# A state-space layer and its experts on one core: readout vector C spread in bfloat16 parts, the sixth state on GpSimd, and a reordered opening

## What is computed

```python
def step(h, inp):                       # per token t
    dA_t, dB_t, x_t, C_t, t = inp
    h = h * dA_t + dB_t * x_t[:, :, None]
    nrm = jnp.sqrt(jnp.sum(h * h, axis=(1, 2), keepdims=True))
    fac = jnp.minimum(20.0 / (nrm + 1e-08), 1.0)
    h = jnp.where(t % 10 == 0, h * fac, h)          # every tenth token the state is rescaled
    y = jnp.einsum('bdn,bn->bd', h, C_t) + D_param * x_t
    return (h, y)
x_out = x_ssm * (gate * jax.nn.sigmoid(gate)) @ W_out.T
# then: softmax router over 16 experts, top 1, capacity 256 tokens each,
# h = relu(tokens @ w1[e]); out = h @ w2[e], weighted by the gate and added to x
```

## Time and profile before

| | before |
|---|---|
| median of 3 runs | 745.5 us (743.75 to 746.16) |
| the profiled execution: device time, and span in the trace | 746.58 us, 744.9 us |
| mean granted clock of TensorE | 0.935 of full |
| busy, share of the span | PE 85%, PEld 63%, DVE 81%, ACT 78%, POOL 81% |
| costliest groups | DVE scans L1360 318.2 us; POOL products L842 299.2 us; ACT tanh L1076 237.5 us; PE state sums L1722 214.5 us; PE spread of C L1712 101.2 us |
| chain that ended last | PE 29%, DVE 20%, POOL 18%, issue 16%, ACT 12%, DMA 3% |
| stages in the trace | first scan at 38.3 us; segments to 618 us; last logits and routing to 653.7 us; experts to 739.3 us |

### The profile page before, as it was taken

The page is one execution under the profiler, slowest core; times in us unless marked ns, Lnnn a source line. Parts: engine busy times, 40 slices in busy tenths (PEclk is TensorE's granted clock), DMA queues, the critical chain, the costliest instruction groups (busy, mean ns, idle before and its releaser), DMA issues.

```text
span 744.9 us, 12724 instructions
## 1 busy us (share of the span) xinstructions
PE 632.3 (85%) x3892; PEld 467.7 (63%) x3892; DVE 601.7 (81%) x972; ACT 582.1 (78%) x1217; POOL 602.4 (81%) x600
## 2 busy tenths in 40 slices
PE   6787899989989998998999899999978885179974
PEld 3335566667667666666667666766767765168864
DVE  5788799999999999999899999999997974742321
ACT  3797989989999999999999998999988642223330
POOL 4288699999999999999899999999897871167775
PEclk9879799999999999999999999999988897579998
DMA  4340333126134322613441352334124302235652
GB/s 119 100 149 2 129 96 112 55 84 192 52 122 141 105 64 79 192 58 109 110 139 45 100 166 86 99 85 148 49 73 135 78 3 65 70 108 181 202 168 66
DMA packets 59168, 77.03 MB, mean 103 GB/s; under 512 B 13514, under 2 KB 46060, under 8 KB 59104
## 3 DMA queue, kind: packets, MB, share of 16 engines
q1 hardware_dynamic: 55328, 69.92, 31.1%
q0 software_dynamic: 2560, 6.08, 2.6%
q10 hardware_dynamic: 1216, 0.27, 0.2%
HBM read 64.70 MB, written 11.77 MB: 103 GB/s over the span
## 4 chain that ended last, share of the span: by engine, by line
PE 29%; DVE 20%; POOL 18%; issue 16%; ACT 12%; DMA 3%; POOLq 0%; SPq 0%; DVEq 0%; ACTq 0%
DVE h L1360 10%; PE ps L1722 9%; POOL h L842 7%; ACT z L1076 6%; PE ps L1615 3%; PE ps L1712 3%; POOL h L856 3%; PE ps L1697 3%; ACT ps L966 2%; POOL nrm L867 2%; PE ps L581 2%; PE ps L594 2%; DVE bst L1244 2%; POOL h L863 1%; DVE h L1334 1%
## 5 line engine op out<-in xcount | busy, mean ns | idle before, releaser
L1360 DVE TENSOR_TENSOR_SCAN h<-ps,h 128x902 f32<-128x902 f32 x204 | 318.2, 1608 | 16.3 <-ACT ps L966 8.4
L842 POOL TENSOR_TENSOR h<-u,scr 128x640 f32<-128x640 f32 x208 | 299.2, 1471 | 1.7
L1076 ACT ACTIVATE z<-dtb,asc 128x240 f32<-128x240 f32 x576 | 237.5, 485 | 1.0 <-DVE dtb L1301 0.7
L1722 PEld LDWEIGHTS ps<-h,ident 128*128 128x128 f32 x1428 | 208.7, 198 | 24.7 <-issue 13.8
L1722 PE MATMUL ps<-h,ident 128*128 128x160 f32 x1428 | 214.5, 310 | 3.6 <-DVE h L1411 3.2
L966 ACT ACTIVATE ps<-z 128x820 f32<-128x820 f32 (+1 forms) x208 | 139.6, 691 | 29.0 <-DVE h L1360 20.4
L1411 DVE TENSOR_TENSOR h<-h,ps 128x800 f32<-128x800 f32 (+4 forms) x161 | 116.5, 725 | 6.7 <-PE ps L1712 5.9
L1712 PE MATMUL ps<-cdg,ones_w 128*128 128x480 f32 x208 | 101.2, 578 | 0.0
L856 POOL TENSOR_TENSOR h<-h,scr 128x800 f32<-128x800 f32 (+1 forms) x52 | 89.7, 1725 | 0.7 <-DVE h L1376 0.7
L1615 PE MATMUL ps<-xnT,wT 128*128 128x488 f32 x144 | 73.7, 624 | 1.1 <-DVE xnT L1472 0.8
L867 POOL TENSOR_TENSOR nrm<-s,half_e 8x1 f32<-8x1 f32 x52 | 33.1, 636 | 46.8 <-DVE s L1323 46.5
(11 more groups left out here) (196 smaller groups left out, 854.1 us busy)
## 6 DMA issues: line engine op xcount, KB each, us to landing
scr<-b_d SPq DMA_DIRECT2D x52, 640.0 KB, 4.4
scr<-c_d SPq DMA_DIRECT2D x52, 200.0 KB, 4.3
z<-in_L_ffn_w_dram SPq DMA_DIRECT2D x32, 256.0 KB, 3.0
xx_d<-xx SPq DMA_DIRECT2D x8, 256.0 KB, 2.0
xxr<-xx_d SPq DMA_DIRECT2D x8, 256.0 KB, 2.6
cdg<-cdg_d SPq DMA_DIRECT2D x52, 37.8 KB
rows_d<-h2b SPq DMA_DIRECT2D x16, 120.0 KB, 2.1
rows_d<-xxr SPq DMA_DIRECT2D x16, 120.0 KB, 2.2
```

Of the source, the lines that this page charges most:

```text
L842: pool.tensor_tensor(o.rearrange("p (n b) t -> p n b t", b=B), us.unsqueeze(1).to_broadcast([P, nn, B, SEG]), bb[:, S % RING, n0 * BS:(n0 ...
L1076: ins = act.activation(zrow[:, k, :, t0:t1], dtb[:, v % 2, hf, :].rearrange("p (b c) -> p b c", b=B)[:, :, 1 + t0:1 + t1], ACT.Tanh, scale ...
L1360: dve.tensor_tensor_scan(hs, region(G)[:, 0:(r1 - r0) * SLOT], hs, 0.0, ALU.mult, ALU.add).then_inc(gscan, 1)
L1722: pe.matmul(ps[:, YB, 0:H * BS], ident[:], hr[:, :, n * B:(n + 1) * B, 0:SEG], start=(n == 0), stop=False)
```

## The change

- **C in bfloat16 parts.** `cs` holds three parts of C. Part 0 is the float32 value; POOL (`split_c`) subtracts from each part its upper half (the bfloat16 that its upper 16 bits are) to get the next. SP stores all three into a block diagonal of 30 partitions, and `spread_c` multiplies their upper halves by bfloat16 ones: one bfloat16 matmul instead of a float32 one. The zeroed area in DRAM and each load grow with it.
- **Six states on GpSimd.** `CP0` is 10 instead of 11. `c_last` multiplies six states (960 elements a partition instead of 800), its addition is gone, and `sum_states` runs 16 matmuls.
- **Stores.** `store_bc` is two: `store_b` at `s`=2, `store_c` at `s`=4. `split_c` is at `s`=3 on POOL, ahead of `products`.
- **First gates from PSUM.** `keep_gate` is gone. ACT takes the gates' tanh from PSUM before the first `steps_tanh`; DVE makes them before the first `take_norm`. `turn_x(1)` uses bank 1, and `project_x(1, .)` runs after `norm_spread(0)`.
- **First products.** POOL waits for DVE's first state, then make_u(0,0), root(0), products of half 0, make_u(0,1), products of half 1.
- **Expert loads.** SP's list is written out: after up(e) comes w1(e+2), after down(e-1) w2(e+1).

```diff
-    CP0 = 11
+    CP0 = 10
     CGRP = [(0, 6), (6, CP0)]
+    PARTS = 3
-        cdg_d = dram("cdg_d", (2, SPW, CP0, CP0, BS))
+        cdg_d = dram("cdg_d", (2, SPW, PARTS * CP0, CP0, BS))
+        ones_b = sb("ones_b", [PARTS * CP0, P], BF16)
-        cs = sb("cs", [NST, SPW * BS])
+        cs = sb("cs", [NST, PARTS, SPW * BS])
+        def upper_half(t):
+            return t.bitcast(BF16).rearrange("p (c two) -> p c two", two=2)[:, :, 1]
...
# sp_tail
-            with sp.Fori(0, E // 2 - 1) as g:
-                for k in range(2):
-                    sp.wait_ge(up_done, 2 * (2 * g + k + 1))
-                    load_w1(2 * g + k + 2, k)
-                    sp.wait_ge(down_done, 2 * g + k + 1)
-                    load_w2(2 * g + k + 2, k)
+            for e in range(E - 1):
+                if e + 2 < E:
+                    sp.wait_ge(up_done, 2 * (e + 1))
+                    load_w1(e + 2, e % 2)
+                if e > 0:
+                    sp.wait_ge(down_done, e)
+                    load_w2(e + 1, (e + 1) % 2)
...
# sync: opening, then the loop
+            store_b(0)
             sp.wait_ge(st_b0, 16)
...
-            store_bc(0)
             spread_b(0)
             spread_b(1)
+            store_c(0)
             spread_cp(0)
...
                 if s == 2 and w + 1 < NWIN:
-                    store_bc(w + 1)
+                    store_b(w + 1)
+                if s == 4 and w + 1 < NWIN:
+                    store_c(w + 1)
...
# store_c
+                sp.wait_ge(cs_split, 2 * (v + 1))
+                for part in range(PARTS):
+                    d = cdg_d[v % 2]
+                    d = bass.AP(tensor=d.tensor, offset=d.offset + part * CP0 * CP0 * BS,
+                                ap=[[(CP0 + 1) * BS, CP0], [PARTS * CP0 * CP0 * BS, SPW], [1, BS]])
+                    sp.dma_start(d, cs[0:CP0, part].rearrange("p (s c) -> p s c", c=BS)).then_inc(st_cd, 16)
...
# gpsimd
-                                   ALU.mult).then_inc(cp_last if S == LS else cp_step, 1)
-                if S == LS:
-                    return
-                pool.wait_ge(cp_step, S + 1)
-                a, b = m[:, :, 0:2 * B, :], m[:, :, 2 * B:4 * B, :]
-                pool.tensor_tensor(a, a, b, ALU.add).then_inc(cp_done, 1)
+                                   ALU.mult).then_inc(cp_last if S == LS else cp_done, 1)
+            def split_c(v):
+                pool.wait_ge(cs_ready, v + 1)
+                at_least(pool, st_cd, 16 * PARTS * v)
+                for part in range(1, PARTS):
+                    src = cs[:, part - 1]
+                    pool.tensor_tensor(cs[:, part], src, upper_half(src), ALU.subtract).then_inc(cs_split, 1)
+                    pool.wait_ge(cs_split, 2 * v + part)
...
+            split_c(0)
+            pool.wait_ge(pre_done, 1 + H)
             make_u(0, 0)
+            root(0)
+            products(0, [0])
             make_u(0, 1)
-
-            root(0)
-            products(0)
+            products(0, [1])
...
+                if s == 3 and v1 < NWIN:
+                    split_c(v1)
                 if s == 4 and v1 < NWIN:
                     make_u(v1, 0)
...
# scalar
             clamp_dt(0)
+            tanh_gate(0, 0)
+            tanh_gate(0, 1)
             act.wait_ge(dt_step, 2)
...
                 if S == 0:
-                    tanh_gate(0, 0)
-                    tanh_gate(0, 1)
                     steps_tanh(w, 1, 0, 12)
...
# vector
-            keep_gate(0)
-            keep_gate(1)
...
+            make_gate(0, 0)
+            make_gate(0, 1)
             take_norm(0)
...
-                if S == 1:
-                    make_gate(0, 0)
-                    make_gate(0, 1)
...
# tensor
-                pe.matmul(ps[:, CBANK[j], 0:(n1 - n0) * BS], ones_w[:], cdg[:, S % 2, n0 * BS:n1 * BS],
+                pe.matmul(ps[:, CBANK[j], 0:(n1 - n0) * BS], ones_b[:],
+                          upper_half(cdg[0:PARTS * CP0, S % 2, n0 * BS:n1 * BS]),
                           start=True, stop=True).then_inc(cb_done, 1)
...
-                sum_states(S, CP0, CP0 + 2)
-                sum_states(S, CP0 + 4, NST)
+                sum_states(S, CP0, NST)
...
             turn_x(1)
-            project_x(1, 0, 0, 2)
             norm_sum(0)
-            project_x(1, 0, 2, 3)
             norm_spread(0)
-            project_x(1, 0, 3, 4)
+            project_x(1, 0)
             project_x(1, 1)
```

More of the change, by code:

```diff
@@ L831, in products @@
                 w, s = place_of(S)
-                pool.wait_ge(u_done, H * (w + 1))
+                pool.wait_ge(u_done, 1 if S == 0 and halves == [0] else H * (w + 1))
                 pool.wait_ge(ld_bb[S % RING], 16 * (S // RING + 1))
@@ L1234, in _ @@
             dve.memset(ones_w[:], 1.0)
+            dve.memset(ones_b[:], 1.0)
             dve.wait_ge(const_dve, 4)
@@ L1457, in _ @@
             dve.wait_ge(w_rest, 1)
-            for G in range(2):
-                ins = dve.memset(region(G)[:, 0:(GRAN[G][1] - GRAN[G][0]) * SLOT].rearrange("p (r c) -> p r c", c=SLOT)[:, :, 0], 0.0)
-            ins.then_inc(da_zero, 1)
             make_xc(0, 0)
@@ L1545, in _ @@
                 else:
-                    c_mult(S, 1, 6, 9)
-                    n0 = 9
+                    c_mult(S, 1, 6, 8)
+                    n0 = 8
                 factor(S + 1)
```

68 lines of the change are left out of this document (31 added, 37 removed).

## The result

The changed kernel takes 740.55 us (median of 8 runs, 737.11 to 744.43) against 745.41 for the kernel before: a ratio of 0.9939, 95% interval 0.9912 to 0.9966. It is faster, by 4.9 us where 10.3 were forecast. The profiled execution took 741.52 us, its span is 739.8 (before 746.58 and 744.9).

A forecast was written before the change was run, and what follows sets the result against it. DVE was taken as the chain, touched once each by ACT, POOL and PE. Terms -3.6 -0.8 -6.9 -0.3 = -11.6, with +1.2 for the clock -10.4: 736.2 us, 735.1 against the median; range 729.5 to 742.5, forecast 733 to 738.5 at 0.50.

The forecast's parts named there:

- (c): Rival: slower than before, PE becomes the bound once two clock falls a window cover `sum_y`; 748.5 us; chance 0.10.
- (d): Rival: it cancels; the split takes 3.0 us, roots at `s`=0 stay late, clock falls too; 744 to 747; chance 0.10.
- Opening, -3.6: First segments: gates from PSUM and early tanh end segment 1's scans earlier (-3.2); with `c_mult` of segments 4 and 5, -3.6.
- DVE's 0.18: Second `c_mult` of each segment loses a state, 0.99 to 0.81 us: 0.18 less, not arriving everywhere.
- the sum for the window: Running total from segment 1's last scan: `s`=2 nothing, `s`=3 +0.26, `s`=4 +0.09 then -0.09, `s`=5 -0.35, `s`=0 -1.15.
- POOL: Six states save 0.57 to 0.6 us a segment, 0.62 gained at `s`=0; split costs 2.4 at `s`=3, factor 0.44 later.
- PE at `s`=5 and `s`=0: Ahead of `norm_sum`, longer `sum_y` (+0.57) and the cheaper first spread (0.33 us) cancel to 0.08 gained.
- The windows, -7.7: Six rounds from the second window to the eighth give -6.9 us, the second window's own `s`=0 gives -0.8.
- The clock, +1.2: PE's falls to half clock at `s`=3: four instead of two, about 1 us each, costing +1.2.
- Rival (b): Clock falls in nearly every window at `s`=3: 4 to 7 us back, 739 to 742; chance 0.17.
- The end, -0.3: Last five segments, bounded by PE's `sum_y`: segment 47 +0.5, then -0.2, -0.2, -0.3 and about -0.1; -0.3 in all.
- The expert stage, 0: New load order ends PE's 0.93 us wait for `w1`, but it lies under POOL's queue: 0, at most 0.5 gained.

The follow-up runs named there:

- experiment 1: New opening alone on the kernel before: 741.09 us, ratio 0.9946; the other way round, the changed kernel with float32 spreads of C: 779.03 us, ratio 1.0458.
- Experiment 2: Kernel before with the new opening, DVE leaving out C's factor for state 10 in every segment but the last: 736.34 us, ratio 0.9873.
- experiment 4: Changed kernel with each split subtraction done twice: 762.09 us, ratio 1.0191; with three of ACT's 64 tanh steps a window left out: 744.97 us, ratio 0.9993.
- experiment 3: Changed kernel with its bfloat16 spread over all 128 rows instead of 30: 736.18 us, ratio 0.9884.
- experiment 6: Changed kernel with the old order of expert weight loads: 738.37 us, ratio 0.9902; kernel before with the new order, twice: 0.9954 and 0.9967.
- experiments 4 and 5: 5: changed kernel, second spread repeated in segments 4-12: 736.36 us; kernel before, new opening, bfloat16 parts: 0.9926; 128 rows, old loads: 0.9886, with `s`=3 matmul 0.9866.
- the filled kernel: Changed kernel with 128 rows, old load order, one more matmul at `s`=3 and repeated second spreads at `s`=4, 5, 0: ratios 0.9844, 0.9844, 0.9855.
- the filled kernel of 30 rows: Changed kernel as measured, new load order, with one more matmul at `s`=3 and repeated second spreads at `s`=4, 5, 0: ratio 0.9882.

## Why the prediction was right or wrong

**Direction and bound: right.** Faster, inside the range, DVE as the chain with three releasers. The rivals (c) and (d) as totals didn't come.

**Opening, -3.6: right in size, not in every step.** -3.97 in the profiles, 4.0 to 4.6 by experiment 1. The third scan of segment 2 starts at 68.23 (forecast near 69), and the wait for the spread went. But DVE waits 3.07 us for PE's `sum_y` in segment 1, which I hadn't seen coming; it cost nothing only because ACT held segment 2 all the same (2.54 of wait there, now 0.52). At the start of segment 3 the gain was 5.02; 1.2 of it went in that segment, where the half clock of the opening covers `sum_y`. That the rest meets the forecast is in part luck.

**DVE's 0.18: right.** 0.81 us for four states. Experiment 2 gives 0.34 a window without the rest of the change; the sum for the window (its figures are running totals) had it arrive at `s`=3, 4, 5 and 0, each with another part of the change beside it, and nothing at `s`=1, where 0.17 arrived which I didn't follow further.

**POOL: right in kind, the split priced too high.** 2.03 us instead of 2.4. The two profiles stand within 0.04 us of each other at the first scan of `s`=2, so the times can be set side by side: the root of `s`=3 starts at 289.53 where I had 289.65. Two errors cancel in that: the split was 0.4 too dear, and the root of `s`=2 didn't start 0.27 earlier (277.38 against 277.39), since it waits for DVE's norm. `s`=2 and `s`=3 together take 23.05 us against 22.87 in this window: +0.18 where I had +0.26 (+0.04 in others, 22.90 against 22.86). The factor comes at 290.36, 0.32 later than before where I had 0.44. The 0.4 of idle time that I expected to see isn't there, since DVE's own work on the gates runs until 290.23; the cover is used up, as experiment 4 shows.

**PE at `s`=5 and `s`=0: the step that failed in the windows.** The prediction said that where the first spread alone stands ahead of `norm_sum`, the two edits cancel, with 0.08 to the good; they add 0.20. The 0.08 didn't even follow from its own price: 0.33 us for the spread gives 0.52 back, 0.05 less than the 0.57 of `sum_y`; it takes a spread of 0.20. `sum_y` was right (+0.53 for 0.57). The spread was priced by columns and type from the routing's sums, whose instructions all have 128 rows; the change's has 30, and that costs 0.10 on the spread, 0.10 on the products ahead of it and 0.11 on the projection behind it. At `s`=0 the same 0.3 makes PE late where POOL's root had been. With 128 rows (experiment 3) the term comes out at 0.09, and a window is 1.08 shorter instead of 0.72. The median, 736.2 against the forecast's 735.1, is near it in part by luck, as the other terms below missed both ways.

**The windows, -7.7: -3.9 without the falls.** 0.43 us are missing in each of six windows, 2.6 in all, and in the main this is PE's part. Another 1.1 comes from taking one window for all: the `s`=0 of the sixth and of the eighth window took 10.55 and 10.20 us before, not the 10.93 of the others, so there was less to gain (now 10.33 in both).

**The clock, +1.2: the second step that failed; the count is luck.** Four falls, as I said (two in the profile of experiment 6, from the same instructions), but in the first two windows at `s`=5 and `s`=0, over `sum_y` or just ahead of it, at 1.7 to 2.4 us each instead of 1 at `s`=3: some +4.8 net in the profiled execution. The forecast itself had falls at `s`=3 alone; a fall over `sum_y` stood only in rival (c), which I had kept for two of them in every window. (Rival (b)'s 739 to 742 counted the 1.2 us of this term twice; by its own terms it is 738 to 741.) Over the runs its share moves: 737.1 us at a mean clock of 0.934, 744.4 at 0.923. The Trainium skill's account (same page, "HAM oscillation — how this bites in real kernels"), that gaps between bursts give the clock back, fits what experiments 4 and 5 show, the fall behind PE's longer wait and the filled kernel without any. It doesn't by itself explain the float32 spreads of experiment 1, with eight falls at a PE busy 429 of 445 us. What it doesn't tell is the price, which went from nothing to 2.7 us by where the fall stood. Why the falls stand in the first two windows stays open.

**The end, -0.3: too small.** -3.02, but 1.6 of it is segment 47 (11.27 instead of 12.90 us), and the new load order on the kernel before, whose segments are the same, had 11.24 there in one execution and 12.90 in another. That part belongs to the execution; the forecast's +0.5 there isn't seen. Another 1.6 is the last three segments, 0.50 to 0.55 each where I had 0.1 to 0.3 (the rest, +0.2, is `s`=3 of the eighth window and its neighbours). DVE's waits of 0.52 for the spread are gone there, and 0.35 to 0.45 for `sum_y` stand in their place. But this too moves with the execution: beside the one with 11.24, the last four segments gain only 0.5 together (45.15 against 45.66 us), so of the 3.0 perhaps 0.5 to 1.3 are the change's (1.3 from the filled kernel of 30 rows, whose segment 47 took 12.91).

**The expert stage, 0: wrong by 0.9 in this comparison.** I had asked what PE's wait was worth and not what the later loads would land beside. The last experts end later, and POOL's last scatters wait 0.84 and 1.24 us for them. That the loads slow the gathers isn't shown: where the two traces have the landing of a late gather (experts 12 and 14 in both), it takes 2.8 to 3.4 us before and after. The cause of the 0.9 stays open.

**Together.** Of the 5.3 us between the forecast's -10.4 and the profiles' -5.06, the windows make +3.8, the clock +3.6, the expert stage +1.0, the opening -0.4 and the end -2.7.

## What to carry over

Price a matmul by its columns, its type and its rows, and together with its neighbours: one of 30 rows among others of 128 costs 0.3 us more in all, which is more than its own columns. A term for a typical window isn't the same in every window: check each. When work is taken off PE or moved around its waits, ask what a fall of its clock would cover at each place: three kernels here that shortened a segment had more falls, one of them came out slower for it, and harmless repeats in PE's waits brought 0.2 to 0.6%, with intervals that overlap. Compare medians and the mean clock of the runs before believing a difference between two profiles.

## What the runs showed of the hardware

- A float32 spread of 480 columns holds PE 0.85 us with 128 rows and 0.99 with 10; in bfloat16 0.21 with 128 rows and 0.31 with 30, with 0.1 us more on the instructions on either side; the load of its stationary operand and the next one then start only with their own matmuls.
- One kernel's executions differ by where the clock falls: 732.8 us at a mean of 0.929 to 740.3 at 0.912 with 128 rows; the kernel before 740.1 to 740.5 at 0.939 to 0.941 and 743.5 to 748.2 at 0.932 to 0.939.
- The expert stage took 84 to 86 us on some chips and 100 to 106 on three others (granted clock in it 0.93 to 0.96 and 0.87 to 0.91, where looked at), while the segments took the same time.
- A subtraction of 16x480 elements on GpSimd with a strided bfloat16 operand takes 1.0 us.
